# A row-threshold search by four scaled steps in place of five bracketed rounds, with the masked scores in PSUM

## The chip, the cores and the metric

The kernel runs on one core of one Trainium2 chip, as one program. The metric is the device time of that program in microseconds. Three runs of the kernel before gave 616.22, 618.63 and 620.35 us (median 618.63).

## The reference, cut to what matters

Two layers follow each other on x, of shape (4, 512, 512): a sparse attention map that is added to x, and a gated mixture of experts (8 experts, the top 2 of each token, and one shared expert). The change lies in the first:

```python
sim = einsum('bhnd,bhmd->bnm', Q, K) / (sqrt(32) * 4)       # 4 batches of 512 x 512
k = int(512 * 0.3)                                          # 153
threshold = top_k(sim, k)[0][:, :, -1:]                     # 153rd largest of each row
A = sigmoid(sim) * (sim >= threshold)
A = (A + swapaxes(A, -1, -2)) * 0.5
x = x + tanh(g_xattn) * ((1 - gamma) * layernorm(x) + gamma * A)
```

So each of 2048 rows of 512 scores needs the exact value of its 153rd largest score. Everything after it (layer norm of the new x, router, shared expert, routed experts) waits for the x that comes out.

## The kernel before

The five engines each run a program written by hand; semaphores order them. There is no scheduler, so the order of the calls in each engine's function is the order of execution. SP issues the loads and stores. A batch is 4 tiles of 128 rows (TPB = 4). Attention of batch 0 runs alone in a prologue, beside the first weight pieces. Then `together(b)` runs three times: the shared expert of batch b and the attention of batch b+1. After these come the shared expert of batch 3, the routing, and 39 steps of routed experts, which hold TensorE from about 360 us to the end.

Weights come through a ring of 4 slots in `stage`, 272 KB a piece. Each piece is loaded (L291), scaled to its high half by ACT (`high_piece`, L586, and L590 for the pieces that GpSimd finishes), and its low half is made by GpSimd (L494) or VectorE (`low_piece`, L1082). Only then is the slot free for the load four pieces later. SP's queue is in order: in the prologue it issues the pieces up to the 23rd before it stores the attended x of batch 0 (L310) and loads x of batch 1 (L305).

The search of one batch, on VectorE with ACT's help:

- GpSimd (`guess`, L439) makes the spread of the row's scores (a power of the variance), a first cut `cur` = mean + 0.5077 spread, and a bracket of two cuts, `lo` and `hi`, with assumed counts 290 and 60.
- `interpolate(b, n)` (L1107), five times: VectorE counts in tiles 0 and 1 how many scores are at or above `cur` (L1114), ACT counts tiles 2 and 3 with a Sign activation (`count`, L625). Eleven tiny VectorE instructions follow (L1117 to L1130): they turn ACT's sums into counts, replace one end of the bracket (L1120, L1121) and interpolate the next cut; the fifth round stops after L1121.
- `thresholds(two)` (L1134), once for each pair of tiles: count again at `hi` and keep the 0/1 flags (L1137), subtract a huge number where the flag is set (L1141), take the 8 largest of what is left (L1146), and pick the one whose place is 152 minus the count (L1149). The masked scores are in SBUF (`masked`, which lies over `junk`, as does `xn`).
- `count_missed` (L1153) counts rows whose rank is not 0 to 7; TensorE sums them (`missed_rows`, L799); `masks` (L1160) reads the sum into a register and, if it is above zero, goes through a fallback that removes the row's largest 8 nineteen times over for all four tiles (L1166 to L1182). Then it multiplies the sigmoids by the mask (L1185).

In `together` on VectorE (L1263): `x_stats` (L1095), round 0, then for each of the 6 pieces u of the shared expert: `shared_hidden` (L1238), round u+1; the two `thresholds` calls come at u = 3, `count_missed` at u = 4, `masks` after u = 5. On ACT (L690): count 0, then for each u: `shared_silu` (L649), count u+1, `shared_high` (L655), `scaled_sigmoid` (L614), `high_piece`, and at u = 3, ahead of silu 4, `base` (L619: (1 + gain) x + shift of the four x tiles). On TensorE (L892): the six `shared_up` (L853), of which piece u waits for the hidden rows of piece u-2, then 12 products of `shared_down` (L870), `missed_rows` (L799), the rest of two output tiles, and the transposes of the masked map (L807).

Of the kernel before, what the change touches and what calls it, by code (L numbers as in the profile page):

```python
# [4 lines left out]
P = 128  # L5
# [33 lines left out]
ROUNDS = 5  # L39
# [10 lines left out]
def build(nc, x, ctx_t, wq_t, wk_t, gates, gate_wt, gate_bias, weights, out, xn_rows):  # L50
# [12 lines left out]
    with ExitStack() as ctx:  # L63
# [77 lines left out]
        lo, hi, cur = (attn_buf(2 * TPB).rearrange("p (a i) -> p a i", a=2) for _ in range(3))  # L141
        steps = attn_buf(3 * TPB).rearrange("p (a i) -> p a i", a=3)
        below, above = sb("below", [P, TPB], U32), sb("above", [P, TPB], U32)
        tmp4 = sb("tmp4", [P, 6, TPB])
        top8, pick8 = (attn_buf(TPB * 8).rearrange("p (i c) -> p i c", i=TPB) for _ in range(2))
        thr = sb("thr", [P, TPB])
        acc = sb("acc", [P, TPB // 2])
# [28 lines left out]
        turn_banks = [pa[0], pa[1], pt_bank, pg[0]]  # L176
        y_banks = [py, pu[0]]
# [227 lines left out]
        def _(pool):  # L405
# [30 lines left out]
            sd, var_e, rstd, step = pt[:, 0, :], pt[:, 1, :], pt[:, 2, :], pt[:, 3, :]  # L436
# [137 lines left out]
        def _(act):  # L574
# [47 lines left out]
            def count(b, n):  # L622
                act.wait_ge(cur_ok, b * ROUNDS + n + 1)
                for i in range(TPB // 2, TPB):
                    act.activation(junk[:, i, :], sim[:, i, :], ACT.Sign, bias=cur[:, 0, i:i + 1], scale=-1.0,  # L625
# [434 lines left out]
        def _(dve):  # L1060
# [46 lines left out]
            def interpolate(b, n):  # L1107

                half = TPB // 2
                if n == 0:  # L1110
                    after(dve, guess_ok, b + 1)
                dve.sem_inc(cur_ok, 1)  # L1112
                for i in range(half):
                    o.mark(dve.tensor_scalar(junk[:, i, :], sim[:, i, :], cur[:, 0, i:i + 1], 0.0, ALU.is_ge, ALU.add,  # L1114
                                             accum_out=cur[:, 1, i:i + 1]))
                after(dve, cnt_sb, (b * ROUNDS + n + 1) * half)
                o.then(dve.tensor_scalar(cur[:, 1, half:], acc[:], -0.5, SEQ / 2.0, ALU.mult, ALU.add))  # L1117
                o.mark(dve.tensor_scalar(above[:], cur[:, 1, :], float(KEEP), None, ALU.is_ge))
                o.then(dve.tensor_scalar(below[:], cur[:, 1, :], float(KEEP), None, ALU.is_lt))
                o.mark(dve.copy_predicated(lo, above[:].unsqueeze(1).to_broadcast([P, 2, TPB]), cur))  # L1120
                o.then(dve.copy_predicated(hi, below[:].unsqueeze(1).to_broadcast([P, 2, TPB]), cur))  # L1121
                if n < ROUNDS - 1:
                    gap, frac, width = tmp4[:, 0, :], tmp4[:, 1, :], tmp4[:, 2, :]
                    o.mark(dve.tensor_tensor(gap, lo[:, 1, :], hi[:, 1, :], ALU.subtract))
# [395 lines left out]
```

## Time and profile before

| | |
|---|---|
| median of three runs | 618.63 us |
| span of the profiled execution | 614.4 us |
| prologue, to the first count of batch 1 | 0 to 96.5 us |
| three passes of `together` | 96.5 to about 290 us |
| shared expert of batch 3, routing, experts | 290 to 614.4 us |
| TensorE busy | 508.7 us, 83% |
| VectorE busy | 374.3 us, 61% |
| ScalarE busy | 268.4 us, 44% |
| GpSimd busy | 236.7 us, 39% |

The profiled execution has no time of its own apart from its span. The median of the runs lies 618.63 - 614.4 = 4.2 us above the span; that is what lies around it (start and end of the program) together with the scatter of the runs. Busy shares are means over stages with different limits, so the stages are to be read one at a time.

### The profile page before, as it was taken

The page shows a single profiled execution, that of the slowest core. Times are in us where ns is not written, and L with a number is a line of the kernel's source. Part 1 is how long each engine was busy: PE and PEld are TensorE (multiplying, and loading weights), DVE is VectorE, ACT ScalarE, POOL GpSimd, SP SyncE. Part 2 cuts the span into 40 slices and gives each one's busy share as a digit, 9 for nine tenths or more (in the row PEclk, how much of TensorE's full clock was granted, in tenths as well). Part 3 has the DMA queues.
Part 4 walks back from the last instruction along what each step waited for, and adds up shares of the span by engine and source line. Part 5 has one row for each costly group of instructions (what it writes and reads, how often), then busy time and mean ns, then how long its engine had stood idle before and what let it go on. Part 6 is the DMA issues. An engine that isn't in the chain of part 4 may idle for free.

```text
span 614.4 us, 11359 instructions
## 1 busy us (share of the span) xinstructions
PE 508.7 (83%) x3169; PEld 287.4 (47%) x3170; DVE 374.3 (61%) x880; ACT 268.4 (44%) x489; POOL 236.7 (39%) x258
## 2 busy tenths in 40 slices
PE   2400768969996999787999589999999999999992
PEld 0100434425543444344556256666666666666661
DVE  0589858997898889985985467533333333333321
ACT  0687496854576467636122345422222232222221
POOL 1226744445342723272023105343443434344332
PEclk9655569979999999986999989999999999999997
DMA  3225374104811372124201779645444453534433
GB/s 107 95 55 162 109 251 141 50 18 138 295 36 36 120 254 78 38 85 166 98 0 41 226 228 244 135 71 95 77 83 88 75 96 68 96 75 83 87 40 47
DMA packets 33204, 65.86 MB, mean 107 GB/s; under 512 B 4177, under 2 KB 4433, under 8 KB 33169
## 3 DMA queue, kind: packets, MB, share of 16 engines
q1 hardware_dynamic: 24432, 44.99, 22.6%
q0 software_dynamic: 8736, 20.45, 18.6%
q8 instruction: 16, 0.26, 0.2%
q14 instruction: 20, 0.16, 0.1%
HBM read 42.10 MB, written 23.33 MB: 106 GB/s over the span
## 4 chain that ended last, share of the span: by engine, by line
PE 52%; DVE 27%; issue 6%; DMA 6%; ACT 4%; POOL 2%; SPq 1%; DVEq 1%; POOLq 0%; ACTq 0%
PE py L1011 12%; PE pg L991 12%; PE pu L992 11%; PE pt_bank L812 3%; DVE w L1114 3%; PE pg L853 3%; PE pu L853 3%; PE pu L870 2%; DVE w L1120 2%; DVE w L1185 2%; DVE w L1141 2%; PE pa L1001 2%; DVE w L1137 2%; ACT w L625 2%; DVE w L1146 2%
## 5 line engine op out<-in xcount | busy, mean ns | idle before, releaser
L991 PE MATMUL pg<-w,x_t 128*128 x468 | 141.7, 314 | 5.4 <-DVE x_t L1447 5.4
L992 PE MATMUL pu<-w,x_t 128*128 x468 | 141.6, 314 | 0.0
L547 POOL DMA_INDIRECT out<-rows,idx x39 | 61.8, 1584 | 138.4 <-ACT rows L752 131.1
L853 PE MATMUL pg<-w 128*128 128x512 f16 (+1 forms) x288 | 80.6, 390 | 3.5 <-DVE work L1238 3.4
L1011 PE MATMUL py<-w,work 128*128 x351 | 82.1, 379 | 0.8 <-DVE work L1442 0.8
L853 PE MATMUL pu<-w 128*128 128x512 f16 (+1 forms) x288 | 79.8, 387 | 0.0
L742 ACT ACTIVATE work<-pg 128x352 f32<-128x352 f32 x39 | 18.1, 463 | 132.9 <-PE pu L992 132.9
L586 ACT ACTIVATE w<-stage 128x544 f16<-128x544 f32 (+1 forms) x80 | 50.8, 647 | 40.9 <-DMA stage<-in_weights 38.9
L494 POOL TENSOR_TENSOR w<-stage,w 128x544 f16<-128x544 f32 (+1 forms) x43 | 53.4, 1252 | 31.1 <-ACT stage L590 29.2
L500 POOL TENSOR_TENSOR work<-work 128x512 f16<-128x512 f32 (+1 forms) x24 | 28.9, 1204 | 94.6 <-ACT work L655 94.3
L1431 DVE SCALAR_TENSOR_TENSOR work<-pu,work 128x352 f32<-128x352 f32 x39 | 20.5, 525 | 65.7 <-ACT work L742 65.7
L991 PEld LDWEIGHTS pg<-w,x_t 128*128 128x128 f16 x468 | 46.0, 98 | 26.6 <-issue 6.3
L992 PEld LDWEIGHTS pu<-w,x_t 128*128 128x128 f16 x468 | 46.0, 98 | 20.5
L1442 DVE COPY work<-pa 128x768 f16<-128x768 f16 x39 | 21.7, 558 | 55.4 <-PE pa L1001 52.1
L1011 PEld LDWEIGHTS py<-w,work 128*128 128x128 f16 x351 | 34.3, 98 | 37.0 <-issue 0.9
L853 PEld LDWEIGHTS pg<-w 128*128 128x128 f16 (+1 forms) x288 | 30.1, 108 | 37.1 <-DVE work L1238 6.7
L853 PEld LDWEIGHTS pu<-w 128*128 128x128 f16 (+1 forms) x288 | 31.2, 108 | 33.5 <-issue 3.3
L799 PE MATMUL pa<-one,missed 128*1 128x1 f32 x8 | 0.8, 163 | 52.1 <-DVEq L1158 52.1
L625 ACT ACTIVATE w<-w 128x512 f16<-128x512 f32 x40 | 28.5, 715 | 26.0 <-DVEq L1112 26.0
L870 PE MATMUL pu<-w,work 128*128 128x512 f16 (+1 forms) x144 | 37.9, 417 | 0.1
L1437 DVE TENSOR_TENSOR work<-work 128x352 f16<-128x352 f32 x39 | 20.4, 524 | 24.6 <-ACT work L747 24.6
L1082 DVE SCALAR_TENSOR_TENSOR w<-stage,w 128x544 f16<-128x544 f32 x37 | 28.2, 792 | 11.9 <-ACT w L586 10.6
(200 smaller groups left out, 845.8 us busy)
## 6 DMA issues: line engine op xcount, KB each, us to landing
stage<-in_weights SPq DMA_DIRECT2D x80, 272.0 KB
out<-rows SPq DMA_DIRECT2D x17, 256.0 KB, 5.4
w<-in_x SPq DMA_DIRECT2D x4, 1024.0 KB, 6.3
out<-w SPq DMA_DIRECT2D x16, 256.0 KB, 3.0
xn_rows<-w SPq DMA_DIRECT2D x16, 256.0 KB, 5.2
rows<-out SPq DMA_DIRECT2D x16, 256.0 KB, 2.9
w<-in_ctx_t SPq DMA_DIRECT2D x4, 256.0 KB, 3.6
out<-rows,idx POOLq DMA_INDIRECT x39, 4.8
```

The lines of the kernel that those rows point to most:

```text
L494: pool.tensor_tensor(w[:, ds(item, 1), 1, n * CHUNK_W:(n + 1) * CHUNK_W], stage[:, n % RING:n % RING + 1, :], w[:, ds(item, 1), 0, n * CHU ...
L500: pool.tensor_tensor(hid_tb[0:m, u, 1, :], hb[0:m, u % 2, :], hid_tb[0:m, u, 0, :], ALU.subtract).then_inc(hlo_sb, 1)
L547: pool.indirect_dma_start(out=out, out_offset=bass.IndirectOffsetOnAxis(ap=idx[:, t:t + 1], axis=0), in_=rows[:, t % 2, :], in_offset=None ...
L586: act.activation(w[:, ds(item, 1), 0, n * CHUNK_W:(n + 1) * CHUNK_W], stage[:, n % RING:n % RING + 1, :], ACT.Copy, scale=W_SCALE).then_in ...
L625: act.activation(junk[:, i, :], sim[:, i, :], ACT.Sign, bias=cur[:, 0, i:i + 1], scale=-1.0, accum_out=acc[:, i - TPB // 2:i - TPB // 2 + ...
L853: mm = pe.matmul(bank_[0:m, :], w[:, half, part, at:at + m], x_tb[:, xpart * KC + k, :], start=(k, part, xpart) == (0, 0, 0), stop=(k, par ...
L870: mm = pe.matmul(bank_[:, :], hid_tb[0:m, u, part, i * P:(i + 1) * P], w[0:m, half, wpart, at:at + C], start=(u, part, wpart) == (0, 0, 0) ...
L991: pe.matmul(pg[p][:, 0:H], lhs, w[:, item, half, at:at + H], start=begin, stop=end)
L992: mm = pe.matmul(pu[p][:, 0:H], lhs, w[:, item, half, at + H:at + 2 * H], start=begin, stop=end)
L1011: mm = pe.matmul(py[:, :], hid_t[:, p, part * JC + j, :], w[:, item, half, at:at + C], start=(j, part, half) == (0, 0, 0), stop=(j, part) ...
L1082: dve.scalar_tensor_tensor(out=w[:, item, 1, n * CHUNK_W:(n + 1) * CHUNK_W], in0=stage[:, n % RING, :], scalar=W_SCALE, in1=w[:, item, 0, ...
L1442: dve.tensor_copy(hid_t[:, p, :, :], hid_banks[p]).then_inc(ht_sb, 1)
```

## The change

The bracket goes. `guess` on GpSimd makes the spread alone, and VectorE makes `cur` = mean + 0.517 spread. A round is now a count and, for each half of the tiles, two instructions: `off` = (count - 148.5) x spread, `cur` = `cur` + `off` x step / 185, with steps 1.0, 0.7, 0.55 and 0.25. There are four rounds. A fifth count, by VectorE in all four tiles, is part of `thresholds`; its flags (`junk`, f16) mask the scores, and the masked scores are written to the PSUM banks pa[0] and pa[1], from which MAX reads them. The picking of the threshold from the 8 largest and the count of missed rows are done for all tiles at once in `count_missed`. In `together`, thresholds of tiles 0 and 1 now stand after hidden piece 3, those of tiles 2 and 3 with `count_missed` after hidden piece 4. On ACT, `base` stands at `u == ROUNDS - 2`, which is now 2.

```diff
-ROUNDS = 5
+STEPS = (1.0, 0.7, 0.55, 0.25)
+ROUNDS = len(STEPS)
+GUESS = 0.517
+SLOPE = 185.0
+AIM = KEEP - 4.5
...
+        below_banks = [pa[0], pa[1]]
...
             def guess(b):
                 after(pool, stats_ok, b + 1)
-                after(pool, cnt_sb, b * ROUNDS * (TPB // 2))
-                mean_s, var_s = mv[:, 0, :, 0], mv[:, 0, :, 1]
-                o.mark(pool.memset(lo[:, 1, :], 290.0))
-                o.mark(pool.memset(hi[:, 1, :], 60.0))
+                var_s = mv[:, 0, :, 1]
                 o.then(pool.tensor_tensor(sd, var_s, half_pow[:, 0, :], ALU.pow))
-
-                bracket = ((cur, 0.5077), (lo, -0.2), (hi, 1.2))
-                for n, (_, z) in enumerate(bracket):
-                    o.mark(pool.tensor_scalar(steps[:, n, :], sd, z, None, ALU.mult))
-                o.wait()
-                for n, (dst, _) in enumerate(bracket):
-                    o.mark(pool.tensor_tensor(dst[:, 0, :], steps[:, n, :], mean_s, ALU.add))
-                o.wait()
                 pool.sem_inc(guess_ok, 1)
...
                 high_piece(n // CHUNKS, n % CHUNKS)
+            base(0, (TPB - 1,))
             for k in range(ROUNDS, FIRST + RING):
...
+            def step_to(two, counted, shift, gain, wait=True):
+                lo, hi = two
+                o.then(dve.scalar_tensor_tensor(out=off[:, lo:hi], in0=counted, scalar=shift, in1=spread[:, lo:hi],
+                                                op0=ALU.add, op1=ALU.mult))
+                o.mark(dve.scalar_tensor_tensor(out=cur[:, lo:hi], in0=off[:, lo:hi], scalar=gain, in1=cur[:, lo:hi],
+                                                op0=ALU.mult, op1=ALU.add))
+
+            def count_above(i):
+                o.mark(dve.tensor_scalar(junk[:, i, :], sim[:, i, :], cur[:, i:i + 1], 0.0, ALU.is_ge, ALU.add,
+                                         accum_out=counts[:, i:i + 1]))
+
+            def search(b, n):
 
                 half = TPB // 2
                 if n == 0:
                     after(dve, guess_ok, b + 1)
+                    o.mark(dve.scalar_tensor_tensor(out=cur, in0=spread, scalar=GUESS, in1=mv[:, 0, :, 0],
+                                                    op0=ALU.mult, op1=ALU.add))
+                o.wait()
                 dve.sem_inc(cur_ok, 1)
                 for i in range(half):
...
+                    count_above(i)
+                o.wait()
+                step_to((0, half), counts[:, 0:half], -AIM, STEPS[n] / SLOPE)
                 after(dve, cnt_sb, (b * ROUNDS + n + 1) * half)
...
+                step_to((half, TPB), acc[:], 2.0 * AIM - SEQ, -0.5 * STEPS[n] / SLOPE)
...
+            def thresholds(b, two):
 
                 o.wait()
...
+                if two[0] == 0:
+                    after(dve, tanh_sb, (b + 1) * TPB)
+                for i in two:
+                    count_above(i)
+                o.wait()
+                made = [o.mark(dve.scalar_tensor_tensor(out=below_banks[i % 2][:, :], in0=junk[:, i, :], scalar=-BIG,
+                                                        in1=sim[:, i, :], op0=ALU.mult, op1=ALU.add)) for i in two]
                 for n, i in enumerate(two):
                     o.wait(made[n])
...
+                    o.mark(dve.max(top8[:, i, :], below_banks[i % 2][:, :]))
 
             def count_missed():
...
+                o.then(dve.tensor_scalar(rank, counts, -1.0, KEEP - 1.0, ALU.mult, ALU.add))
+                o.then(dve.tensor_tensor(hot8, iota_col[:, 0:8].unsqueeze(1).to_broadcast([P, TPB, 8]),
+                                         rank.unsqueeze(2).to_broadcast([P, TPB, 8]), ALU.is_equal))
+                o.then(dve.tensor_scalar(spare8, hot8.rearrange("p i c -> p (i c)"), -1.0, float(TPB), ALU.mult, ALU.add,
+                                         accum_out=missed[:]))
                 dve.sem_inc(miss_ok, 1)
+                o.then(dve.tensor_tensor(hot8, hot8, top8, ALU.mult))
+                o.then(dve.tensor_reduce(thr[:], hot8, AX.X, ALU.add))
...
                     if u + 1 < ROUNDS:
-                        interpolate(b + 1, u + 1)
-                    if u + 2 == ROUNDS:
-                        thresholds((0, 1))
-                        thresholds((2, 3))
+                        search(b + 1, u + 1)
                     if u + 1 == ROUNDS:
+                        thresholds(b + 1, (0, 1))
+                    if u == ROUNDS:
+                        thresholds(b + 1, (2, 3))
                         count_missed()
```

How VectorE's instructions of the end of a search stand in `together`, before. L1238 is a hidden piece of the shared expert (the 4th here, then the 5th and the 6th), L1114 the two counts of the last round:

```order
L1238 SCALAR_TENSOR_TENSOR work<-pu,work 128x512
L1114 TENSOR_SCALAR w<-w 128x512 x2
...
L1137 TENSOR_SCALAR w<-w 128x512 x2
L1141 SCALAR_TENSOR_TENSOR w<-w 128x512 x2
L1143 TENSOR_SCALAR tmp<-w 128x2
L1146 MAX w<-w 128x8 x2
L1149 SCALAR_TENSOR_TENSOR w,thr<-iota_col,tmp,w 128x8 x2
...
L1238 SCALAR_TENSOR_TENSOR work<-pu,work 128x512
L1155 TENSOR_SCALAR tmp<-tmp 128x4
L1156 SCALAR_TENSOR_TENSOR tmp,missed<-tmp 128x4
```

The same place now; L1233 is the hidden piece (again 4th, 5th), L1110 a count:

```order
L1233 SCALAR_TENSOR_TENSOR work<-pu,work 128x512
L1110 TENSOR_SCALAR w<-w 128x512 x2
L1139 SCALAR_TENSOR_TENSOR pa<-w 128x512 x2
L1143 MAX w<-pa 128x8 x2
L1233 SCALAR_TENSOR_TENSOR work<-pu,work 128x512
L1110 TENSOR_SCALAR w<-w 128x512 x2
L1139 SCALAR_TENSOR_TENSOR pa<-w 128x512 x2
L1143 MAX w<-pa 128x8 x2
L1146 TENSOR_SCALAR tmp<-w 128x4
L1147 TENSOR_TENSOR w<-iota_col,tmp 128x32
L1149 TENSOR_SCALAR w,missed<-w 128x32
```

The last search round between the 4th hidden piece and the masking is gone, and the 5th hidden piece has moved up between the two pairs of tiles.

ACT in `together` around `base`, before: L649 is silu (3rd, 4th, 5th piece), L625 the counts of rounds 3 and 4, L619 `base`:

```order
L649 ACTIVATE work<-pg 96x512
...
L625 ACTIVATE w,acc<-w 128x512 x2
...
L649 ACTIVATE work<-pg 128x512
...
L625 ACTIVATE w,acc<-w 128x512 x2
...
L619 ACTIVATE w<-w,pt 128x512 x4
...
L649 ACTIVATE work<-pg 128x512
```

And now: L643 is silu (3rd, 4th, 5th piece), L619 the count of round 3, L613 `base`:

```order
L643 ACTIVATE work<-pg 96x512
...
L619 ACTIVATE w,acc<-w 128x512 x2
...
L613 ACTIVATE w<-w,pt 128x512 x4
...
L643 ACTIVATE work<-pg 128x512
...
L643 ACTIVATE work<-pg 128x512
```

The four instructions of `base` stood ahead of the silu of the 5th piece; now they stand ahead of that of the 4th.

## Rows read from the trace of the kernel before

**Rows 1.** Window: us, busy of PE PEld DVE ACT POOL, PEclk, DMA, GB/s

```profile
96.50:130.90 34.40, 26.68 (x122) 12.41 (x120) 32.17 (x103) 23.41 (x48) 11.86 (x15) 0.96 0.24 66
```

**Rows 2.** Waits of PE, 96 to 290 us: total, times, longest

```profile
PE pa L799 <- DVEq L1158: 14.2, 3, 4.8
PE pg L853 <- DVE work L1238: 3.4, 5, 1.7
```

**Rows 3.** Timeline of DVE: batch 1's search, and batch 2's first count (start us, us, what)

```profile
96.48 0.75 DVE L1114 TENSOR_SCALAR_CACHE_REDUCE w<-w 128x512 f16<-128x512 f32 x1 [0.37 <-DVE mv L1089]
...
100.02 0.69 DVE L1238 SCALAR_TENSOR_TENSOR work<-pu,work 128x512 f32<-128x512 f32 x1 [0.22 <-DVE w L1130]
...
102.43 1.07 DVE L1120 COPY_PREDICATED w<-above,w 128x8 f32<-128x8 uint32 x1
...
104.49 1.12 DVE L1130 TENSOR_TENSOR w<-tmp,w 128x4 f32<-128x4 f32 x1
...
162.68 0.75 DVE L1114 TENSOR_SCALAR_CACHE_REDUCE w<-w 128x512 f16<-128x512 f32 x1 [0.36 <-DVE mv L1089]
```

**Rows 4.** Timeline of POOL in the same round

```profile
102.32 1.16 POOL L500 TENSOR_TENSOR work<-work 128x512 f16<-128x512 f32 x1 [3.02 <-ACT work L655]
104.38 1.22 POOL L494 TENSOR_TENSOR w<-stage,w 128x544 f32 x1 [0.91 <-ACT stage L590]
```

**Rows 5.** Timeline of ACT, the same round, then the end of the search

```profile
100.10 0.72 ACT L625 ACTIVATE w<-w 128x512 f16<-128x512 f32 x1 [1.58 <-DVEq L1112]
...
103.98 0.58 ACT L649 ACTIVATE work<-pg 128x512 f32<-128x512 f32 x1
...
121.35 2.91 ACT L619 ACTIVATE w<-w,pt 128x512 f32<-128x512 f32 x4
```

**Rows 6.** Timeline of PE: last piece, the wait for the missed rows, the next pass

```profile
118.14 0.85 PE L853 MATMUL pg<-w 128*96 128x512 f16 x3 [0.44 <-DVE work L1238]
...
123.36 2.76 PE L870 MATMUL py<-w,work 128*128 128x512 f16 x12
130.89 0.19 PE L799 MATMUL pa<-one,missed 128*1 128x1 f32 x2 [4.77 <-DVEq L1158]
...
157.47 0.81 PE L853 MATMUL pg<-w 128*128 128x512 f16 x3
```

**Rows 7.** Groups of DVE by form, 96 to 131 us: busy, mean ns

```profile
L1114 DVE TENSOR_SCALAR_CACHE_REDUCE w<-w 128x512 f16<-128x512 f32 x10 | 7.0, 740 | 0.4 <-DVE mv L1089 0.4
L1146 DVE MAX8 w<-w 128x8 f32<-128x512 f32 x4 | 2.6, 679 | 0.0
L1127 DVE SCALAR_TENSOR_TENSOR tmp<-w,tmp 128x4 f32<-128x4 f32 x4 | 0.7, 163 | 0.1
```

**Rows 8.** One line's DVE instructions over the span: ns min/median/max, first and last start

```profile
L1141 DVE SCALAR_TENSOR_TENSOR w<-w x16: 679/685/1699, 47.9 to 258.8; 128x512 f32<-128x512 f32 x16
L1245 DVE SCALAR_TENSOR_TENSOR rows<-py,cst,rows x8: 736/748/751, 138.2 to 355.0; 128x512 f32<-128x512 f32 x8
```

**Rows 9.** Timeline of ACT in the prologue

```profile
36.76 0.72 ACT L625 ACTIVATE w<-w 128x512 f16<-128x512 f32 x1
...
38.89 0.64 ACT L586 ACTIVATE w<-stage 128x544 f16<-128x544 f32 x1
...
40.20 0.72 ACT L625 ACTIVATE w<-w 128x512 f16<-128x512 f32 x1
```

**Rows 10.** Timeline of DVE in the prologue

```profile
46.60 0.74 DVE L1137 TENSOR_SCALAR_CACHE_REDUCE w<-w 128x512 f32<-128x512 f32 x1
...
50.60 1.17 DVE L1143 TENSOR_SCALAR tmp<-w 128x2 f32<-128x2 f32 x1
...
60.26 1.08 DVE L1156 SCALAR_TENSOR_TENSOR tmp<-tmp 128x4 f32<-128x4 f32 x1
```

**Rows 11.** Chain that ended last, 75 to 97 us: start us, us, what

```profile
78.91 1.77 POOL w L494
...
86.72 6.48 DMA w<-in_x
```

More of the change, by code:

```diff
@@ L140, in build @@
         pt = sb("pt", [P, 8, TPB])
-        lo, hi, cur = (attn_buf(2 * TPB).rearrange("p (a i) -> p a i", a=2) for _ in range(3))
-        steps = attn_buf(3 * TPB).rearrange("p (a i) -> p a i", a=3)
-        below, above = sb("below", [P, TPB], U32), sb("above", [P, TPB], U32)
+        cur, counts, off = attn_buf(TPB), attn_buf(TPB), attn_buf(TPB)
         tmp4 = sb("tmp4", [P, 6, TPB])
-        top8, pick8 = (attn_buf(TPB * 8).rearrange("p (i c) -> p i c", i=TPB) for _ in range(2))
+        top8, hot8 = (attn_buf(TPB * 8).rearrange("p (i c) -> p i c", i=TPB) for _ in range(2))
+        spare8 = attn_buf(TPB * 8)
         thr = sb("thr", [P, TPB])
+        spread = pt[:, 0, :]
         acc = sb("acc", [P, TPB // 2])
@@ L435, in _ @@
             pool.wait_ge(cst_ok, 1)
-            sd, var_e, rstd, step = pt[:, 0, :], pt[:, 1, :], pt[:, 2, :], pt[:, 3, :]
+            sd, var_e, rstd, step = spread, pt[:, 1, :], pt[:, 2, :], pt[:, 3, :]
             o = Order(pool, pool_ch)
@@ L1121, in interpolate @@
[L1121 to L1124, printed above, removed]
-                    o.then(dve.tensor_tensor(width, hi[:, 0, :], lo[:, 0, :], ALU.subtract))
-                    o.then(dve.reciprocal(gap, gap))
-                    o.then(dve.scalar_tensor_tensor(out=frac, in0=lo[:, 1, :], scalar=KEEP - 4.0, in1=gap,
-                                                    op0=ALU.subtract, op1=ALU.mult))
-                    o.then(dve.scalar_tensor_tensor(out=frac, in0=frac, scalar=0.98, in1=width, op0=ALU.min, op1=ALU.mult))
-                    o.then(dve.tensor_tensor(cur[:, 0, :], frac, lo[:, 0, :], ALU.add))
@@ L1132, in _ @@
[L1132 to L1138 removed]
+                step_to((half, TPB), acc[:], 2.0 * AIM - SEQ, -0.5 * STEPS[n] / SLOPE)
+            rank = tmp4[:, 3, :]
+            def thresholds(b, two):
+                o.wait()
+                if two[0] == 0:
[5 more added lines that the diff above has]
+                                                        in1=sim[:, i, :], op0=ALU.mult, op1=ALU.add)) for i in two]
@@ L1139, in thresholds @@
                 for n, i in enumerate(two):
                     o.wait(made[n])
-                    made[n] = o.mark(dve.scalar_tensor_tensor(out=masked[:, i % 2, :], in0=masked[:, i % 2, :], scalar=-BIG,
-                                                              in1=sim[:, i, :], op0=ALU.mult, op1=ALU.add))
-                o.mark(dve.tensor_scalar(rank[:, two[0]:two[1] + 1], hi[:, 1, two[0]:two[1] + 1], -1.0, KEEP - 1.0, ALU.mult, ALU.add))
-                for n, i in enumerate(two):
-                    o.wait(made[n])
-                    made[n] = o.mark(dve.max(top8[:, i, :], masked[:, i % 2, :]))
@@ L1147, in thresholds @@
-                for n, i in enumerate(two):
-                    o.wait(made[n])
-                    o.mark(dve.scalar_tensor_tensor(out=pick8[:, i, :], in0=iota_col[:, 0:8], scalar=rank[:, i:i + 1],
-                                                    in1=top8[:, i, :], op0=ALU.is_equal, op1=ALU.mult,
-                                                    accum_out=thr[:, i:i + 1]))
-            def count_missed():
-                o.wait()
-                o.then(dve.tensor_scalar(miss, rank, 0.0, None, ALU.is_lt))
-                o.then(dve.scalar_tensor_tensor(out=miss, in0=rank, scalar=7.5, in1=miss, op0=ALU.is_gt, op1=ALU.add,
-                                                accum_out=missed[:]))
+                    o.mark(dve.max(top8[:, i, :], below_banks[i % 2][:, :]))
@@ L1264, in together @@
                 x_stats(b + 1)
-                interpolate(b + 1, 0)
+                search(b + 1, 0)
                 for u in range(UPS):
```

21 lines of the change are left out of this document (5 added, 16 removed).

## Prediction

> **What bounds the kernel now.** I read the windows by stage first. From 96.5 to 130.9 us, the search of batch 1, VectorE is busy 32.17 of 34.4 us, TensorE 26.68, ACT 23.41 [rows 1]: VectorE sets the pace there, although over the whole span it looks idle 39% of the time. Then the waits of TensorE, 96 to 290 us: three times (once a pass of `together`) it stands up to 4.8 us, 14.2 in all, at L799, until the missed rows are counted [rows 2]. The wait ends a stretch of work that was finished long before: 12 products at 123.36 for 2.76 us, then nothing until 130.89 [rows 6]. So what shortens the search moves the end, up to the point where something else is last. The chain of waits from 75 to 97 us shows the same for the prologue: the row scalars that follow the attention of batch 0 on GpSimd, a low half of a weight piece at 78.91, stores, and the load of x at 86.72 [rows 11] lead to the first count of batch 1 at 96.48 [rows 3]. After 290 us the change touches nothing; that part should shift as a block.
>
> **One round in `together`.** From one hidden piece (100.02) the instructions go on to L1130 at 104.49 + 1.12 and the next hidden piece at 105.8, so a round takes VectorE 5.8 us. The two counts take some 1.4 (0.74 each, started 0.67 apart) [rows 7]. Most of the rest should be eleven tiny instructions of 0.16 [rows 7], about 1.8 us; but L1120 and L1130 take 1.07 and 1.12 [rows 3]. They end when GpSimd's subtractions end (102.32 + 1.16, 104.38 + 1.22) [rows 4]: an instruction with two inputs in SBUF waits while GpSimd works. The Trainium skill states this ("SBUF — State Buffer", Who interferes with whom): VectorE with two SBUF inputs against a GpSimd instruction that reads SBUF, the later one blocks until the other is through; the trace agrees.
>
> Now four instructions of that kind replace the eleven: 0.65 us, so VectorE's round falls to 0.6 (hidden piece) + 1.4 + 0.1 (ACT's two counts end last) + 0.65 = 2.8 us free, 4 to 5 if it meets GpSimd twice. What is late next? ACT: from its counts at 100.10 to the end of the following silu at 103.98 + 0.58 = 104.56 it works without a gap, 4.46 us [rows 5], and the next round's counts start when VectorE has that silu. TensorE needs 5.2 us a piece (the last of batch 0 from 118.14 to 123.36), and in the later passes it starts some 5 us before the first count (157.47 against 162.68) [rows 3, 6]. So I take ACT's 4.46 us as the round, and the tiny instructions, met or not, hide under it (slack 1.6 us).
>
> **The end of a search, counted from its first count at 0.** Count 1 at 2.45 (before: 100.10 - 96.48 = 3.6), count 2 at 7.0, count 3 at 11.6. Then silu 3 is due on ACT: another 4.46, but `base` now stands ahead of it, 2.91 us in the trace [rows 5], 2.8 in sequence. Silu 3 ends at 18.9, hidden piece 3 at 19.6. VectorE, which has had its last cut since 14.5, waits for that. Thresholds of tiles 0 and 1: counts 1.4, two maskings 1.2, two MAX 1.2 (0.68 each, 0.6 apart [rows 7]), waits 0.1: 3.9, and 0.4 more since a masking (two SBUF inputs) meets GpSimd's low half of piece 3: 23.9. Hidden piece 4: 24.5. Tiles 2 and 3: 3.9, 28.4, perhaps 0.3 of meeting. Three small instructions of `count_missed`: 0.65. The matmul for the missed rows is then at 29.4; before, at 130.89 - 96.48 = 34.4 [rows 3, 6]. Gain 5.0. Against it: VectorE makes `cur` itself ahead of the first count (0.25), and after the matmul's release two more small ones (0.3). Net 4.5 us a pass, 13.5 for three. The removed bracket on GpSimd gives nothing here, since `x_stats` hides it.
>
> **Masked scores in PSUM.** No row of before shows a VectorE write of this kind to PSUM, or MAX out of it. Bounds from SBUF: a masking takes 0.68 us free and 1.70 when GpSimd holds it up; with an input from PSUM a similar one takes 0.75 [rows 8]. So an end of 0.1 dearer for each of 8, 0.8 us a batch, and an end of 1.0 cheaper for each of 4 maskings if the place of the output were what GpSimd contends for. I take no change, since the two inputs (flags and scores) remain in SBUF and the free row is nearest. By the rule of the Trainium skill named above, it is the inputs that count, and the masking would still be held up; only MAX is untouched, as it was. The end "cheaper" would bring the sum down by up to 4 us a batch, and the rule speaks against it.
>
> **The prologue.** Here the round is ACT's already: counts at 36.76 and 40.20 with no gap between, 3.44 us, made of counts 1.5, a quarter of `base` 0.7 (2.91 / 4 [rows 5]), and a weight piece for the rest, of which its high half is 0.64 [rows 9]. So the shorter VectorE chain is worth nothing a round, except in round 1, which starts after 31.8 instead of 33.3 (a stalled small instruction delayed it). Counts then at 31.8, 35.25 and 38.7; the last ends at 40.2. VectorE's `low_piece(0, 3)` must wait for that piece's high half on ACT: 40.2 + 0.7 (`base`) + 0.64 = 41.6, then 0.7. Thresholds start at 42.3 in place of 46.60 [rows 10]: 4.3 us. In the pairs, L1143 (1.17, held up) and L1149 (0.3) go from the first, 0.3 from the second, and `count_missed`, whose L1156 took 1.08 [rows 10], becomes 0.3 shorter if it isn't held up: 4.3 + 1.4 + 0.3 + 0.2 = 6.2, less 0.1 behind the matmul: 6.1 us. Does the weight ring keep up? Every slot is freed by work that moves forward too (low pieces 3 and 7 on VectorE 4 to 6 us earlier), and I find the 14th piece's low half, which stands ahead of GpSimd's addition, at about 57.9, with the first masked tiles at 57 to 58. It fits, barely; nothing is left over there; that is an estimate, made of ACT's pieces at 1.3, low halves at 1.2 to 1.6, and some 3 us a load. From there the chain [rows 11] shifts whole.
>
> **Sum.** 6.1 + 13.5 = 19.6 us off the profiled execution's 614.4, so a span of 594.8. The median of the runs stands 4.2 us above that span, so 599.0 us.
>
> **Rivals.** *TensorE last.* If ACT's `base` isn't in the way (VectorE and ACT overlap better than I draw), TensorE is: six pieces of 5.2 us, starting 5.2 before the first count, then 2.65 of products, puts L799 at 28.7 at the earliest in the later passes, and the gain is 5.7 less 0.55, 5.1 net a pass. With 7.5 in the prologue (no stalls), 22.8 in all: 595.8 us. For it: the waits for hidden pieces are small, 3.4 us in all [rows 2]. Against: the row of `base` [rows 5].
>
> *The ring is last in the prologue.* If loads of weight pieces set the start of GpSimd's addition or of the stores, the 6.1 go, and 13.5 stay: 605 us. For it: the chain passes over a weight piece at 78.91 [rows 11]. Against: that piece waited for GpSimd's own row scalars, not for a load.
>
> *Each edit worth its VectorE time.* A round of 5.8 us removed and 3 us from each of four others would be 17 us a pass, 50 in three: some 560 us. TensorE's six pieces already forbid it; this is the sum to mistrust.
>
> *The fallback runs.* The old search kept a bracket, the new one trusts a slope of 185 counts per spread. If in a batch a single row of 512 ends with a count outside 145 to 152, VectorE goes through L1166 to L1182: nineteen times MAX and a replacement for each of four tiles. With MAX at 0.68 [rows 7] and the replacement taken at the same (no row shows one; between 0.68 and 1.70, the ends of a masking [rows 8]), some 1.5 us a turn with the waits, 4 x 19 x 1.5 + 4 x 1.5 = 120 us a batch, up to 190: 719 us or more, slower by 16%. Against it: following both rules in plain arithmetic on the reference's inputs gives last counts of 146 to 152 before and 145 to 152 after, none outside, though 5 rows of 2048 stand on the two edge values; after three of the four steps one row in each of three batches would still have been outside. And no row of before lies in those lines. That the last step is small (0.25) keeps rounding from mattering.
>
> **How the numbers follow.** Forecast as above 0.66 (599). TensorE last 0.17 (596). Ring last 0.13 (605). Fallback 0.03 (719). VectorE time in full, or another faster mix, 0.01. The range: per pass 3.3 to 5.3 us (two held-up instructions that ACT's round doesn't hide; PSUM 0.8 dearer; or TensorE's limit), prologue 3.5 to 8. That is 13.4 to 23.9 off, and 2 us for the scatter of the runs: 593 to 606.5 us. A measurement of this kernel can tell about 1%, 6 us, from no change. Every case but the fallback gives at least 12: faster 0.95, same 0.02, slower 0.03.
>
> **What would show it.** Right: the first count of batch 1 at about 90.4; L799 of the first pass 29 to 30 us after it; ACT without a gap between counts and silu in `together`; hidden piece 3 waiting for silu 3 behind `base`, with VectorE idle some 4 to 5 us there; TensorE's wait at L799 under 1 us in the later passes; the stretch after 290 us unchanged in length. Wrong: VectorE busy to the end of the search (then maskings or MAX are dearer than I take them), x of batch 1 not earlier than 90, or any instruction in L1166 to L1177.

## Result and profile after

Four runs of the changed kernel gave 597.36 to 601.43 us, median 599.81; the kernel before, timed beside it, gave 616.22 to 620.35 us, median 618.0. The ratio is 0.9702 [0.9672, 0.9733], 18 us less. The forecast was 599.0 us.

| | before | after |
|---|---|---|
| median | 618.0 us | 599.81 us |
| span of the profiled execution | 614.4 us | 595.3 us |
| first counts of batches 1, 2, 3 | 96.48, 162.68, 228.34 | 90.79, 153.07, 213.99 |
| VectorE busy | 374.3 us, 880 instructions | 343.4 us, 708 instructions |
| TensorE busy | 508.7 us | 505.0 us |

The difference of the spans is 19.1 us: 5.7 before the first of those counts, 3.9 and 4.7 in the two whole passes, and 4.75 from the third first count to the end (386.06 and 381.31 us). Of these 4.75, 4.0 lie in the third pass, up to the routing's first instruction on VectorE (at 289.18 before, 270.83 now). The other 0.75 is in the stretch that the change doesn't touch (325.22 and 324.47 us); the kernel with `base` moved, below, takes 325.25 there, so I count it as scatter of the execution.

The waits of TensorE from 90 to 275 us, which answer to [rows 2] (total, times, longest):

```profile
PE pa L802 <- DVE w L1180: 5.8, 3, 2.5
...
PE pa L794 <- DVEq L1151: 3.3, 3, 2.4
PE pg L848 <- DVE work L1233: 2.6, 2, 1.8
```

The wait for the missed rows (L799 before, L794 now) fell from 14.2 to 3.3 us. A new one is at its head: the transposes at L802 wait for the multiplication by the mask.

Timeline of VectorE: the first two first counts, to be held against [rows 3]:

```profile
90.31 0.32 DVE L1118 SCALAR_TENSOR_TENSOR w<-pt,mv 128x4 f32<-128x4 f32 x1 [0.24 <-DVE mv L1084]
90.79 0.75 DVE L1110 TENSOR_SCALAR_CACHE_REDUCE w<-w 128x512 f16<-128x512 f32 x1 [0.16 <-DVE w L1118]
...
153.07 0.74 DVE L1110 TENSOR_SCALAR_CACHE_REDUCE w<-w 128x512 f16<-128x512 f32 x1 [0.17 <-DVE w L1118]
```

Timeline of TensorE: the matmul for the missed rows in the three passes, against the one at 130.89 in [rows 6]:

```profile
120.65 0.19 PE L794 MATMUL pa<-one,missed 128*1 128x1 f32 x2 [2.38 <-DVEq L1151]
...
182.00 0.19 PE L794 MATMUL pa<-one,missed 128*1 128x1 f32 x2 [0.48 <-DVEq L1151]
...
243.35 0.19 PE L794 MATMUL pa<-one,missed 128*1 128x1 f32 x2 [0.48 <-DVEq L1151]
```

It comes 29.9, 28.9 and 29.4 us after the first count of its pass.

Timeline of ACT in the first pass, against [rows 5]:

```profile
93.12 0.72 ACT L619 ACTIVATE w<-w 128x512 f16<-128x512 f32 x1 [0.29 <-DVEq L1121]
...
97.00 0.58 ACT L643 ACTIVATE work<-pg 128x512 f32<-128x512 f32 x1
97.68 0.72 ACT L619 ACTIVATE w<-w 128x512 f16<-128x512 f32 x1
...
102.24 0.72 ACT L619 ACTIVATE w<-w 128x512 f16<-128x512 f32 x1
...
106.12 2.92 ACT L613 ACTIVATE w<-w,pt 128x512 f32<-128x512 f32 x4
108.94 0.57 ACT L643 ACTIVATE work<-pg 128x512 f32<-128x512 f32 x1
```

The counts start 4.56 us apart and nothing stands idle between them: ACT is the round. Then `base` (L613), and silu 3 only behind it. VectorE at the same time:

```profile
95.41 1.10 DVE L1104 SCALAR_TENSOR_TENSOR w<-acc,pt 128x2 f32<-128x2 f32 x1
97.61 0.69 DVE L1233 SCALAR_TENSOR_TENSOR work<-pu,work 128x512 f32<-128x512 f32 x1 [0.91 <-ACT work L643]
...
109.55 0.69 DVE L1233 SCALAR_TENSOR_TENSOR work<-pu,work 128x512 f32<-128x512 f32 x1 [3.73 <-PE pu L848]
...
111.61 1.79 DVE L1139 SCALAR_TENSOR_TENSOR pa<-w 128x512 f32<-128x512 f16 x2
113.31 1.28 DVE L1143 MAX8 w<-pa 128x8 f32<-128x512 f32 x2
```

One small instruction a round is still held up (1.10 us), but 0.91 us of idle time behind it hides that. Hidden piece 3 comes after 3.73 us of idling. The releaser printed there is TensorE, but what ends on it at 109.51 is the piece after this one, while silu 3 ends on ACT at the same time. That it was ACT is shown by the first experiment: with silu 3 moved ahead, hidden piece 3 starts at 106.75, in the middle of that TensorE piece.

### The profile page after: what moved, and what is told of

It reads as the page before. It is cut to its first block, busy times and chain, and to the rows that moved or that the text cites. A ratio compares the mean times of both kernels' runs of the same rounds, so it can differ in the third digit from the quotient of the medians.

```text
span 595.3 us, 11124 instructions
## 1 busy us (share of the span) xinstructions
PE 505.0 (85%) x3169; PEld 287.2 (48%) x3170; DVE 343.4 (58%) x708; ACT 262.7 (44%) x473; POOL 231.9 (39%) x226
## 3 DMA queue, kind: packets, MB, share of 16 engines
q0 software_dynamic: 8736, 20.45, 19.1%
## 4 chain that ended last, share of the span: by engine, by line
PE 58%; DVE 18%; ACT 7%; issue 6%; DMA 6%; POOL 2%; SPq 1%; DVEq 1%; POOLq 0%; ACTq 0%
PE py L1006 12%; PE pg L986 12%; PE pu L987 12%; PE pg L848 5%; PE pu L848 5%; PE pt_bank L807 4%; DVE w L1180 3%; DVE pa L1139 3%; DVE w L1110 2%; PE pa L996 2%; PE pu L865 2%; DVE w L1143 1%; ACT w L619 1%; DVE w L1187 1%; ACT w L613 1%
## 5 line engine op out<-in xcount | busy, mean ns | idle before, releaser
L1006 PEld LDWEIGHTS py<-w,work 128*128 128x128 f16 x351 | 34.3, 98 | 37.0 <-issue 0.9
L865 PE MATMUL pu<-w,work 128*128 128x512 f16 (+1 forms) x144 | 34.7, 391 | 0.1
L1110 DVE TENSOR_SCALAR_CACHE_REDUCE w<-w 128x512 f16<-128x512 f32 x48 | 33.7, 739 | 1.2 <-DVE w L1118 0.7
L865 PE MATMUL py<-w,work 128*128 128x512 f16 (+1 forms) x144 | 34.1, 388 | 0.2 <-DVE rows L1240 0.2
```

The costliest lines, as they stand in the source:

```text
L865: mm = pe.matmul(bank_[:, :], hid_tb[0:m, u, part, i * P:(i + 1) * P], w[0:m, half, wpart, at:at + C], start=(u, part, wpart) == (0, 0, 0) ...
L1006: mm = pe.matmul(py[:, :], hid_t[:, p, part * JC + j, :], w[:, item, half, at:at + C], start=(j, part, half) == (0, 0, 0), stop=(j, part) ...
```

## Experiments

Each ratio is to the kernel before, timed beside it on the same chip (medians 618.44, 618.25 and 617.18 us on three occasions). Unless said otherwise the edit is to the changed kernel.

**`base` behind silu 4.**

```diff
-                    if u == ROUNDS - 2:
+                    if u == ROUNDS:
                         base(b + 1)
```

> The changed kernel, but in together ACT's base stands at u = 4 (behind silu 4) and not at u = 2 (ahead of silu 3). Theory (ACT's round and base hold the end of the search): silu 3 ends 2.9 us earlier, the missed-rows matmul comes about 27.1 us after the first count in the first pass (now 29.9) and, since TensorE's products then end last, at about 28.5 in the later two (now 28.9 and 29.3); hidden piece 5 is then done ahead of the matmul, some 0.7 us more. In all 4 to 5.5 us faster than the changed kernel, about 594.5 us (ratio to before 0.961 to 0.964). Rival (TensorE or VectorE already bounds the pass, base costs nothing): within 1 us of 599.8, ratio 0.970.

Measured: 590.45 us (590.08 to 592.64), ratio 0.957 [0.954, 0.960]. Right in direction, and larger than the expected 4 to 5.5 us: 9 us by the medians, 8 by the ratios, 6.6 by the spans of the profiled executions (of the changed kernel the profiled one was the fastest of four). TensorE's timeline:

```profile
117.78 0.19 PE L794 MATMUL pa<-one,missed 128*1 128x1 f32 x2 [0.48 <-DVEq L1151]
...
175.94 2.76 PE L865 MATMUL py<-w,work 128*128 128x512 f16 x12
178.63 0.19 PE L794 MATMUL pa<-one,missed 128*1 128x1 f32 x2
...
237.65 0.19 PE L794 MATMUL pa<-one,missed 128*1 128x1 f32 x2
```

In the first pass silu 3 comes 2.8 us earlier, and so does the matmul. The first pass becomes 2.84 us shorter by that (first counts 90.81, 150.25, 208.85). In the later passes L794 has no wait any more: TensorE's pieces and products are last, as in the prediction's rival. That limit left 0.5 us to gain in the second pass, and it became 2.32 us shorter. The rest is behind the matmul. The masks of that pass in the changed kernel:

```profile
184.35 5.54 DVE L1180 SCALAR_TENSOR_TENSOR w<-w,thr 128x512 f32<-128x512 f32 x4 [0.96 <-DVE missed_i L1157]
```

and with `base` behind silu 4:

```profile
179.96 4.78 DVE L1180 SCALAR_TENSOR_TENSOR w<-w,thr 128x512 f32<-128x512 f32 x4 [0.96 <-DVE missed_i L1157]
```

VectorE finishes early enough to have made hidden piece 5 already, so the masks start 1.3 us after the matmul, not 2.35 (182.00 to 184.35). GpSimd's low half of that piece (178.95, 1.16 us) is nearly over by then: the first mask takes 0.75 us, and the four 4.78, not 5.54. These two, 1.0 and 0.76, and the 0.55 ahead of the matmul are the 2.32 us. A wait measured at one instruction had understated the cost of what is late.

**Both `thresholds` calls at the old places** (u = 2 in a four-round search; `count_missed` at u = 3).

```diff
-                    if u + 1 == ROUNDS:
-                        thresholds(b + 1, (0, 1))
-                    if u == ROUNDS:
-                        thresholds(b + 1, (2, 3))
+                    if u + 2 == ROUNDS:
+                        thresholds(b + 1, (0, 1))
+                        thresholds(b + 1, (2, 3))
+                    if u + 1 == ROUNDS:
                         count_missed()
```

> The changed kernel with both thresholds calls at the old place relative to the rounds (u + 2 == ROUNDS, now behind hidden piece 2) and count_missed behind hidden piece 3. Theory (VectorE works some 8.5 us on the thresholds ahead of hidden piece 3, TensorE's sixth piece waits for that one, so the products end at about 32 us and the matmul with them): 2.2 us a pass, 6 to 7 us slower than the changed kernel, 606 us, ratio 0.980. Rival (where thresholds stand among the hidden pieces is free, since VectorE's work is the same): within 1 us of 599.8, ratio 0.970.

Measured: 605.34 us, ratio 0.9783 [0.9763, 0.9803], as expected: some 5 us of the 18 hang on the new places (5.5 by the medians, 5.0 by the ratios). The waits of TensorE in this run:

```profile
PE pg L848 <- DVE work L1233: 13.5, 4, 5.2
...
PE pa L802 <- DVE w L1180: 2.6, 3, 1.1
```

The thresholds are ready early, no wait for the missed rows is left, and TensorE waits 13.5 us for hidden pieces instead: hidden piece 3 comes at 115.09, behind 8.0 us of thresholds (from 107.08).

**`base` late in the prologue** (all four tiles behind the eighth weight piece, none between the counts).

```diff
                 count(0, n)
-                if n:
-                    base(0, (n - 1,))
...
-            base(0, (TPB - 1,))
...
+                if k == CHUNKS - 1:
+                    base(0)
```

> The changed kernel, but in the prologue ACT's four base instructions stand behind the 8th weight piece and not one behind each round. Theory (the prologue's round is ACT's: 1.4 counts, 0.7 base, 1.3 weight piece): rounds of 2.75 instead of 3.35 us, the weight piece that VectorE waits for 2.7 us earlier, thresholds begin about 2 us earlier; some of it lost to the weight ring: 1 to 2 us faster, ratio 0.967 to 0.969. Rival (the ring of weight loads sets when the masks can be used, it fits barely): within 0.5 us, ratio 0.970.

Measured: 599.05 us, ratio 0.9706 [0.9677, 0.9735]: no difference that can be told from the changed kernel's 0.9702. Yet the search itself did become shorter. VectorE's timeline (the first row shown is `low_piece(0, 3)`, behind which the thresholds start at 38.03, in place of 41.22, of which 1.08 is an earlier start of the whole search):

```profile
37.39 0.73 DVE L1076 SCALAR_TENSOR_TENSOR w<-stage,w 128x544 f16<-128x544 f32 x1
38.03 0.74 DVE L1109 TENSOR_SCALAR_CACHE_REDUCE w<-w 128x512 f16<-128x512 f32 x1
...
47.77 1.15 DVE L1145 TENSOR_SCALAR tmp<-w 128x4 f32<-128x4 f32 x1
48.95 1.16 DVE L1146 TENSOR_TENSOR w<-iota_col,tmp 128x32 f32<-128x32 f32 x1
...
52.28 1.48 DVE L1179 SCALAR_TENSOR_TENSOR w<-w,thr 128x512 f32<-128x512 f32 x1 [0.43 <-issue]
...
88.74 0.75 DVE L1109 TENSOR_SCALAR_CACHE_REDUCE w<-w 128x512 f16<-128x512 f32 x1 [0.17 <-DVE w L1117]
```

Of 2.1 us at the thresholds (3.2 less the earlier start) 1.0 us is left at the first count of batch 1 (88.74 against 90.79, less 1.08). Two small instructions met GpSimd (1.15 and 1.16 us), the masks took 6.44 us in place of 5.71, and the load of x 7.86 in place of 7.39. And 1 us is within the scatter of the runs.

**Both moves of `base`,** the two diffs above together.

> The changed kernel with both moves of `base` on ACT: in `together` behind silu 4 (alone 590.45 us) and in the prologue all four behind the eighth weight piece (alone 599.05 against 599.81). Theory: the two gains lie in different stretches and add, but that of the prologue is mostly given back by GpSimd's addition, the masks and the load of x: 589.5 to 590.5 us, ratio 0.953 to 0.956, first count of batch 1 at 88.5 to 90. Rival: the 2 us by which the first count came earlier is real and only the scatter of the starts hid it: 588.5 us, 0.952.

Measured: 591.52 us (588.88 to 593.32), ratio 0.9582 [0.9554, 0.9610]. It lies above the range given, and the first count of batch 1 comes at 90.56, not at 88.5 to 90. The time can't be told from that of the move in `together` alone (0.957), so the move in the prologue is worth nothing that can be measured. That makes the kernel with one move, 0.957, the version to keep; it beats both kernels.

**Masked scores in SBUF.**

```diff
-                    count_above(i)
+                    o.mark(dve.tensor_scalar(masked[:, i % 2, :], sim[:, i, :], cur[:, i:i + 1], 0.0, ALU.is_ge, ALU.add,
+                                             accum_out=counts[:, i:i + 1]))
...
-                made = [o.mark(dve.scalar_tensor_tensor(out=below_banks[i % 2][:, :], in0=junk[:, i, :], scalar=-BIG,
+                made = [o.mark(dve.scalar_tensor_tensor(out=masked[:, i % 2, :], in0=masked[:, i % 2, :], scalar=-BIG,
...
-                    o.mark(dve.max(top8[:, i, :], below_banks[i % 2][:, :]))
+                    o.mark(dve.max(top8[:, i, :], masked[:, i % 2, :]))
```

> The changed kernel with the fifth count's flags and the masked scores in SBUF (f32, as before) in place of f16 flags and PSUM. Theory (what GpSimd contends for is the second SBUF input, so the place of the output is free): maskings 0.68 us free and held up as before, MAX 0.68; within 1 us of the changed kernel, ratio 0.969 to 0.972. Rival (PSUM output spares the contention): 0.5 to 1 us more for each pair that meets GpSimd, 2 to 4 us slower, ratio 0.974 to 0.977.

Measured: 599.62 us, ratio 0.9715 [0.9682, 0.9747]. VectorE's groups, first those of the changed kernel (busy us, mean ns of one):

```profile
L1139 DVE SCALAR_TENSOR_TENSOR pa<-w 128x512 f32<-128x512 f16 x16 | 16.0, 1043 | 0.3
L1143 DVE MAX8 w<-pa 128x8 f32<-128x512 f32 x16 | 10.3, 681 | 0.0
```

and those with the scores in SBUF:

```profile
L1140 DVE SCALAR_TENSOR_TENSOR w<-w 128x512 f32<-128x512 f32 x16 | 16.1, 1045 | 0.3
L1144 DVE MAX8 w<-w 128x8 f32<-128x512 f32 x16 | 10.2, 677 | 0.0
```

The means are equal, held-up cases included (685 to 1767 ns and 679 to 1758). Writing to PSUM neither costs nor frees anything here. (The flags are f32 in this run and f16 in the changed kernel, so the two are taken together.)

**Four more small instructions in each round.**

```diff
                 step_to((half, TPB), acc[:], 2.0 * AIM - SEQ, -0.5 * STEPS[n] / SLOPE)
+                for k in range(4):
+                    o.then(dve.reciprocal(tmp4[:, 0, :], tmp4[:, 0, :] if k else spread))
```

> The changed kernel with four more tiny dependent VectorE instructions (reciprocals of 128x4, 0.18 us each and 0.2 with the wait) at the end of each of the 16 rounds. Theory (ACT's 4.46 us round covers VectorE's 3.7 in together, its 3.35 us round in the prologue): the 0.8 us shows only in the first round of a pass, where VectorE is last, so 0.8 x 3 and up to 0.4 in the prologue: 2 to 3 us slower, ratio 0.973 to 0.975. Rival (each VectorE instruction counts): 16 x 0.8 = 12.8 us slower, ratio 0.990.

Measured: 602.02 us, ratio 0.975 [0.9719, 0.9781], 2.2 us more than the changed kernel. Sixty-four instructions, 0.2 us each with its gap, are 13 us of VectorE time over four batches, and 2.2 appear in the medians, 4.9 in the spans of the two profiled executions (595.3 and 600.2). In `together`:

```profile
98.55 0.60 DVE L1129 RECIPROCAL tmp<-tmp 128x4 f32<-128x4 f32 x3
99.35 0.69 DVE L1235 SCALAR_TENSOR_TENSOR work<-pu,work 128x512 f32<-128x512 f32 x1 [0.20 <-ACT work L643]
```

The idle 0.91 us in front of the hidden piece has shrunk to 0.20. So most of the chain of small instructions hides under ACT, and the cover ends about there: the two whole passes are 1.8 and 1.9 us longer, more than the 0.8 expected of each.

**No last step,** so that in some batches a row ends outside the eight and the fallback runs.

```diff
-STEPS = (1.0, 0.7, 0.55, 0.25)
+STEPS = (1.0, 0.7, 0.55, 0.0)
```

> The changed kernel with the last step 0 (1.0, 0.7, 0.55, 0.0): by arithmetic on the reference's inputs one row in each of three batches then lies outside counts 145 to 152, so the fallback runs three times. Theory (price of the prediction, 120 us a batch, up to 190): 960 us, up to 1170. If the count of rows is off on the chip, 720 (one batch) or 840 (two) instead; if none, 600.

Measured, in one run: 1051.29 us. VectorE's groups:

```profile
L1169 DVE MAX8 w<-w 128x8 f32<-128x512 f32 x228 | 158.5, 695 | 93.3 <-DVE w L1171 90.8 <-DVE w L1166 2.5
L1171 DVE MATCH_REPLACE8 w<-w 128x512 f32<-128x512 f32 x228 | 154.1, 676 | 0.0
...
L1171 DVE MATCH_VALUE_LOAD w<-w 128x8 f32 x228 | 21.0, 92 | 7.8
```

228 is 3 batches of 4 tiles by 19 turns, so the fallback ran in three of four batches, for (1051.3 - 599.8) / 3 = 150.5 us each; 76 turns of 1.88 us are 143 of them. That agrees with the prediction's count of one row outside in each of three batches after three steps; in the profile of the changed kernel no instruction lies in the fallback.

**Five cheap rounds, and four dear ones.** The change does two things to the search, cheaper rounds and fewer. Each alone:

```diff
-STEPS = (1.0, 0.7, 0.55, 0.25)
+STEPS = (1.0, 0.7, 0.55, 0.25, 0.25)
...
-            base(0, (TPB - 1,))
```

> The changed kernel with five scaled steps (the last, 0.25, twice), so the cheap round with the old number of rounds; thresholds then stand behind hidden pieces 4 and 5, base at u = 3. Theory (a round costs ACT's time, 3.35 us in the prologue, and the end of a search in together moves from 29.4 to about 33.8 us after its first count): 14 to 15 us slower than the changed kernel, about 614 us, ratio to before 0.993. So the cheaper round alone is worth some 4 us. Rival (most of the gain is the small instructions taken out of each round): 605 us or less, ratio under 0.98.

Measured: 612.32 us, ratio 0.9909 [0.9887, 0.9931]. Near what was expected. Of its 6 us, 4.6 are in the prologue (first count of batch 1 at 91.89), 1.0 of them since the whole search starts earlier in this execution (27.69 against 28.71). The two whole passes take 65.83 and 64.58 us (before: 66.20 and 65.66). With `ROUNDS` the places in `together` move too, and what is late is hidden piece 4, behind `base`:

```profile
115.20 0.69 DVE L1232 SCALAR_TENSOR_TENSOR work<-pu,work 128x512 f32<-128x512 f32 x1 [3.72 <-ACT work L643]
```

The other half, on the kernel before (bracketed rounds; the fallback is left out):

```diff
-ROUNDS = 5
+ROUNDS = 4
...
+            base(0, (TPB - 1,))
...
-                with dve.If(any_missed > 0):
+                with dve.If(any_missed > P * TPB):
...
-                    if u + 2 == ROUNDS:
-                        thresholds((0, 1))
-                        thresholds((2, 3))
                     if u + 1 == ROUNDS:
+                        thresholds((0, 1))
+                    if u == ROUNDS:
+                        thresholds((2, 3))
                         count_missed()
```

> The kernel before with its bracket and its dear rounds, but four of them, and thresholds, count_missed and base at the new places; two rows of 2048 then lie outside the 8 largest, their threshold is wrong and the fallback is left out. Theory: prologue 3.4 us shorter; in together the dear round is VectorE's, 5.8 us, so the fourth count starts at 15.2 instead of 11.6, the missed-rows matmul comes at about 33 us (before 34.4, changed 29.4): 610.5 us, ratio 0.987. Rival (the number of rounds is all): 600 us, ratio 0.970.

Measured: 616.4 us (10 runs), ratio 0.9974 [0.9948, 0.9999]. A miss by 6 us: a round fewer gave 2. Timeline of VectorE in the first pass, then TensorE's waits:

```profile
110.94 0.16 DVE L1122 COPY_PREDICATED w<-below,w 128x8 f32<-128x8 uint32 x1
114.93 0.69 DVE L1239 SCALAR_TENSOR_TENSOR work<-pu,work 128x512 f32<-128x512 f32 x1 [3.83 <-ACT work L649]
```

```profile
PE pa L800 <- DVEq L1159: 9.2, 3, 3.5
PE pg L854 <- DVE work L1239: 9.2, 6, 2.7
```

The search is over at 111.1 and then VectorE idles 3.83 us for silu 3, which `base` holds back; the freed round had become a wait, and TensorE, for which hidden pieces had cost 3.4 us [rows 2], waits 9.2 for them. The passes are even 0.7 us longer than before (66.89 and 66.39 us); what was gained lies in the prologue. So I moved `base` in both kernels with bracketed rounds.

**Four dear rounds, and five, with `base` behind silu 4.** First the four:

```diff
-                    if u == ROUNDS - 2:
+                    if u == ROUNDS:
                         base(b + 1)
```

> The kernel before with four bracketed rounds (two rows' thresholds may come out otherwise; 616.4 us with `base` ahead of silu 3), now with `base` behind silu 4. Theory: the four dear rounds gained little because hidden piece 3 waited for silu 3 behind `base` (VectorE idle 3.83 us at 114.93) just where the fifth round had been. With `base` out of the way silu 3 comes at 111.5 instead of 114.3 and the rest of the pass follows: 2.2 to 2.8 us a pass, 608 to 610 us, ratio 0.984 to 0.987. Rival: the maskings and TensorE's products end the pass anyway, so the stall at hidden piece 3 is only moved: 615 to 616.5 us, 0.995 to 0.997.

Measured: 607.88 us, ratio 0.9848 [0.9821, 0.9875], as expected. Hidden piece 3 now waits 1.02 us:

```profile
111.57 0.16 DVE L1122 COPY_PREDICATED w<-below,w 128x8 f32<-128x8 uint32 x1
112.74 0.69 DVE L1239 SCALAR_TENSOR_TENSOR work<-pu,work 128x512 f32<-128x512 f32 x1 [1.02 <-ACT work L649]
```

And the kernel before, five rounds, with `base` behind silu 4 likewise:

```diff
-                    if u == ROUNDS - 2:
+                    if u == ROUNDS - 1:
                         base(b + 1)
```

> The kernel before with `base` one piece later (behind silu 4, ahead of silu 5, where it stood behind the piece of u = 3). Theory: the place of `base` matters only where ACT is what VectorE waits for. In the kernel before VectorE works on thresholds without a gap from 121.08 to 129.80 and takes hidden piece 4 after them, so nobody waits for silu 4: 617.5 to 619 us, ratio 0.998 to 1.001. Rival: the late `base` is worth some 2 to 3 us a pass whatever the search is: 610 to 612 us, 0.988.

Measured: 617.7 us (12 runs; before 617.18), ratio 1.0002 [0.9984, 1.0021]. Nothing, as expected; TensorE's waits are those of [rows 2]:

```profile
PE pa L799 <- DVEq L1158: 14.2, 3, 4.8
```

Put together, as ratios to the kernel before:

| | `base` ahead of the silu | `base` behind silu 4 |
|---|---|---|
| five dear rounds | 1 | 1.0002 |
| five cheap rounds | 0.9909 | not run |
| four dear rounds | 0.9974 | 0.9848 |
| four cheap rounds | 0.9702 (the change) | 0.957 |

Nothing here adds. ("Cheap" stands for all that goes with the new round: its first guess, the place of the masked scores, and the picking of the thresholds for all tiles at once. No run takes these apart, but for the place of the scores.) Cheap rounds are worth 6 us with five rounds and 17 with four; a round fewer is worth 2 us or 9 with dear rounds, as `base` lies, and 13 with cheap ones; and the place of `base` is worth 0 us while VectorE sets the pace, and about 8 once it doesn't (0.9974 to 0.9848, 0.9702 to 0.957). The changed kernel's 18 us are a product of both halves and of the new places.

## Why the prediction was right, and where not

*What bounds the kernel.* Right: VectorE's search set the end of each pass and the start of the first. The stretch after the passes was to keep its length; it came out 0.75 us shorter, within the scatter of executions.

*The round in `together`.* Forecast: ACT's 4.46 us; measured 4.56. Forecast that held-up small instructions hide (slack 1.6): one a round is held up, and 0.91 us is over.

*The end of the search.* Forecast 29.4 us from the first count to the matmul for the missed rows, a gain of 5.0. Measured 29.9, 28.9, 29.4 against 34.4, 34.3, 33.7: gains of 4.5, 5.4 and 4.4. Hidden piece 3 waits behind `base` as drawn, with VectorE idle for 3.7 us and not 4 to 5. In the later passes TensorE is only 0.5 us from being last.

*Net of a pass.* Forecast 4.5; measured 3.9, 4.7 and 4.0. From the matmul to the next first count I had 0.55 us more than before (0.3 for two small instructions, 0.25 for `cur`); it is 0.6 and 0.7 (32.4 and 32.0 us, before 31.8 and 31.3). Three passes: 12.7 us against 13.5.

*The prologue.* Forecast 6.1, measured 5.7, and that near only by luck, out of two errors that nearly cancel. The thresholds started at 41.22, earlier than the forecast 42.3: ACT's second counts began at 31.10, not 31.8, and the next two came 3.35 us apart, not 3.45, so `low_piece(0, 3)` started at 40.58, not 41.6. VectorE in the prologue:

```profile
41.22 0.74 DVE L1110 TENSOR_SCALAR_CACHE_REDUCE w<-w 128x512 f16<-128x512 f32 x1
...
42.67 3.39 DVE L1139 SCALAR_TENSOR_TENSOR pa<-w 128x512 f32<-128x512 f16 x2
...
49.25 2.35 DVE L1139 SCALAR_TENSOR_TENSOR pa<-w 128x512 f32<-128x512 f16 x2
...
55.61 5.71 DVE L1180 SCALAR_TENSOR_TENSOR w<-w,thr 128x512 f32<-128x512 f32 x4
```

The masks then started 7.9 us earlier than before (63.47), 1.8 more than I had. But "From there the chain shifts whole" failed: 2.2 us were given back on the way to the first count. The masks took 5.71 us instead of 4.76, and the last two links, which answer to [rows 11], were dearer:

```profile
75.18 4.43 DMA out<-w
79.77 7.39 DMA w<-in_x
```

The load of x took 7.39 us instead of 6.48, the store before it 4.43 instead of 3.90. `cur`, which I had counted in each pass, I left out here: with it VectorE's last instructions before the first count take 0.35 us more. Against these stands 0.55 us that came back, since the weight piece of [rows 11] took 1.22 us on the chain instead of 1.77. The masks are held up by GpSimd. Why the transfers took longer was not tested; the trace shows only that beside the load of x the queue moved more weights (2.20 MB in all over those 7.4 us, 2.01 MB over the 6.5 before, at 296 and 312 GB/s).

*PSUM.* Taken as no change, with 0.8 us a batch dearer or 4 us cheaper as ends: no change, to 4 ns in the means. The cheaper end is refuted, and with it the thought that the place of the output is what meets GpSimd. The Trainium skill ("SBUF — State Buffer", Who interferes with whom) lets two SBUF inputs decide; the maskings, held up alike with their output in either memory, agree. No run here takes an input of theirs out of SBUF.

*The sum.* 19.6 us forecast, 19.1 measured in the spans, of which 18.35 lie where the change works. The 4.2 us that I put around the span was wrong in its make-up: the profiled execution took 597.36 us with a span of 595.3, so 2.1 us lie around it, and the rest had been the scatter between that execution and the median. The spans of the four runs go from 595.3 to 599.4 us. It cost nothing here, but by luck: in both kernels the profiled execution was among the fastest, so the difference of the spans stands for that of the medians (19.1 and 18.2). Two slips in the sums cost nothing either: by its own terms the range ends at 618.6 - 13.4 + 2 = 607.2 us, not 606.5, and a rival of 50 us off would be 568 us, not 560.

*Rivals.* TensorE last (0.17) was not this kernel, but it is what comes next: with `base` out of the way L794 waits for nothing in the later passes. Its price, 595.8, was too high by 5 us against 590.45. Some 2.4 us of that are the 4.2 around the span, which was 1.85 in that run. In the spans it was 2.9 too high: the three passes gained 6.8, 7.1 and 6.2 us (the last taken to the end) instead of 5.1 each, because I took the wait at L799 as all that lateness costs, and the prologue 5.7 instead of 7.5. The fallback's price, 120 to 190 us a batch, holds 150.5.

## What to carry to other kernels

When the engine that sets the pace gets faster, look at once at what the next engine does in the stretch that is now late: here 2.9 us of work a pass that nobody waited for (moving it in the kernel before: 1.0002) became 8 us of the new kernel's time over three passes. Price the parts of a change together where they share one pace-setter, since each alone may show almost nothing (0.9909 and 0.9974, together 0.9702). And follow a shift to its end: a start that is 8 us earlier arrived as 6, and a matmul that is 0.5 us earlier as 2.3.

## What was unexpected of the hardware

- A small instruction with one tensor input is held up too. The `tensor_scalar` on 128x4 takes 0.14 us in the first pass of the changed kernel; in the kernel with `base` behind silu 4, which moves it against GpSimd, it is

```profile
116.17 1.04 DVE L1146 TENSOR_SCALAR tmp<-w 128x4 f32<-128x4 f32 x1
```

and GpSimd is at work for just that time:

```profile
116.03 1.15 POOL L494 TENSOR_TENSOR work<-work 128x512 f16<-128x512 f32 x1 [4.36 <-ACT work L649]
```

For the rounds in `together` I had given only instructions with two SBUF inputs as those that wait, though L1143 in [rows 10], held up to 1.17 us, has one. The section of the Trainium skill named above has it, in its lines on the modes of VectorE that use both ports: plain `tensor_scalar` can be among those that exclude GpSimd. The 1.04 us here and the 1.15 in the prologue with `base` late agree; the counts, which write out an accumulator, stayed between 0.73 and 0.75 us throughout, as it says of that form.
- The same two maskings cost from 1.30 to 3.39 us in one execution of the changed kernel, as they meet GpSimd or not. An instruction that is moved by a few microseconds can change its price by more than its own length.
- In the fallback, a turn takes 1.9 us, of which the replacement is 0.68 and MAX 0.70; 0.4 us of it is VectorE's wait for its own result.
